# Attention probabilities transposed on TensorE: eight 128x128 transposes per unit, or sixteen in two row halves of the array

## The reference, cut to what matters

```python
scores = jnp.einsum('bhqd,bhkd->bhqk', q, k)
attn = jax.nn.softmax(scores / math.sqrt(DK), axis=-1)
out = jnp.einsum('bhqk,bhkd->bhqd', attn, v)
...
return out @ wo + bo
```

## Time and profile before

| | |
|---|---|
| time, median of 3 runs | 607.12 us (605.61 to 608.26) |
| the profiled execution | 603.87 us |
| its span, first to last instruction | 602.1 us |
| PE busy, PEld busy | 555.6 us (92%), 509.2 us (85%) |
| DVE, ACT, POOL busy | 459.0 us (76%), 302.1 us (50%), 335.5 us (56%) |
| mean granted clock of TensorE | 0.990 |

### The profile page before, as it was taken

How to read it: one execution, slowest core, us unless ns; L and a number is a source line. 1 busy time by engine, 2 the same in 40 slices (tenths; PEclk the granted TensorE clock), 3 DMA queues, 4 the chain that set the end, 5 groups by cost and what they waited for, 6 DMA issues and landing times.

```text
span 602.1 us, 22151 instructions
## 1 busy us (share of the span) xinstructions
PE 555.6 (92%) x9632; PEld 509.2 (85%) x9632; DVE 459.0 (76%) x902; ACT 302.1 (50%) x647; POOL 335.5 (56%) x665
## 2 busy tenths in 40 slices
PE   6699999999998999999999988899999989999984
PEld 6588798989897988988989878789898979898874
DVE  4977877777777767677767798888888878888862
ACT  6365666575866666557565742242322424222252
POOL 1613535354436353648457496877676555465635
PEclk9979999999999999999999998999999999999999
DMA  8900000000111100000000000000000000000000
GB/s 244 282 2 3 3 2 2 2 4 2 37 37 37 38 4 2 3 2 3 2 3 3 2 3 1 1 3 2 7 7 7 7 10 7 7 7 7 5 12 14
DMA packets 10975, 12.44 MB, mean 21 GB/s; under 512 B 1024, under 2 KB 8704, under 8 KB 10880
## 3 DMA queue, kind: packets, MB, share of 16 engines
q1 hardware_dynamic: 10880, 11.04, 6.2%
HBM read 9.99 MB, written 1.05 MB: 18 GB/s over the span
## 4 chain that ended last, share of the span: by engine, by line
PE 60%; DVE 19%; ACT 8%; POOL 8%; issue 4%; DMA 1%; SPq 0%; POOLq 0%; ACTq 0%; DVEq 0%
PE ps_p L366 10%; PE ps_p L481 10%; PE ps_p L367 8%; PE ps_p L368 8%; PE ps_s L395 5%; PE ps_o L410 5%; PE ps_p L455 3%; ACT probs L574 3%; DVE top L698 3%; DVE probs L721 3%; PE ps_p L503 2%; ACT vv L549 2%; DVE rope_b L655 2%; ACT headsT L568 2%; PE ps_s L388 2%
## 5 line engine op out<-in xcount | busy, mean ns | idle before, releaser
L568 ACT ACTIVATE headsT<-ps_o 128x512 f32<-128x512 f32 x96 | 52.2, 596 | 206.9 <-PE ps_o L410 206.9
L481 PE MATMUL ps_p<-wo,headsT 128*128 128x128 f32 x768 | 94.1, 276 | 2.3 <-ACT headsT L568 1.3
L481 PEld LDWEIGHTS ps_p<-wo,headsT 128*128 128x128 f32 x768 | 89.7, 192 | 3.6 <-DVE rope_a L655 1.5
L709 DVE TENSOR_REDUCE total<-probs 128x16 f32<-128x1024 f32 x48 | 58.4, 1216 | 36.2 <-ACT probs L574 36.2
L698 DVE TENSOR_REDUCE top<-ps_s 128x8 f32<-128x512 f32 x96 | 61.7, 685 | 26.3 <-PE ps_s L395 26.1
L847 POOL TENSOR_TENSOR small<-mv,epsilon 128x1 f32<-128x1 f32 x48 | 17.9, 374 | 113.0 <-DVE mv L691 111.8
L721 DVE TENSOR_TENSOR probs<-probs,rinv 128x512 f32<-128x512 f32 x96 | 68.2, 713 | 0.0
L574 ACT ACTIVATE probs<-probs 128x512 f32<-128x512 f32 x96 | 61.2, 638 | 12.7 <-DVE probs L702 12.7
L366 PE MATMUL ps_p<-xT_hi,wq_hi 128*128 128x256 f32 x192 | 59.5, 310 | 5.9 <-DVE xT_lo L642 3.3
L455 PE MATMUL ps_p<-eye,probs 128*128 128x128 f32 x384 | 53.9, 275 | 9.7 <-ACT vv L549 2.9
L549 ACT ACTIVATE vv<-ps_p 128x512 f32<-128x512 f32 x96 | 57.5, 599 | 9.3 <-PE ps_p L450 9.1
(11 more groups left out here) (144 smaller groups left out, 1480.3 us busy)
## 6 DMA issues: line engine op xcount, KB each, us to landing
out<-y_out SPq DMA_DIRECT2D x16, 64.0 KB, 1.5
X<-in_x SPq DMA_DIRECT2D x1, 768.0 KB, 8.0
across<-in_across SPq DMA_DIRECT2D x1, 704.0 KB, 10.4
wq_raw<-in_L_xattn_sa_wq SPq DMA_DIRECT2D x2, 256.0 KB, 3.1
wk_raw<-in_L_xattn_sa_wk SPq DMA_DIRECT2D x1, 512.0 KB, 5.1
wv_raw<-in_L_xattn_sa_wv SPq DMA_DIRECT2D x1, 512.0 KB, 7.7
wo<-in_L_xattn_sa_wo SPq DMA_DIRECT2D x1, 512.0 KB, 8.8
wo<-in_L_xattn_ca_wo SPq DMA_DIRECT2D x1, 512.0 KB, 10.1
```

The lines of the kernel that those rows point to most:

```text
L481: last = mm(bank[:, 0:E], headsT[:, p, :, :].rearrange("r b q -> r (b q)"), wo[:, layer % 2, p, :], start=(p == 0), stop=(p == PAIRS - 1))
L568: nc.scalar.activation(headsT[:, :, b, :], ps_o[b][:, :].rearrange("r (p q) -> r p q", q=S), ACT.Copy)\
```

## The change

The ring's wait is moved into a helper, and the two fills P0 and P1 are written by one loop. Instead of 8 transposes of 128 rows, each into one bank for a pair of heads, it issues 16 of 64 rows: batch 0 (rows 0 to 63) goes into one bank, batch 1 (rows 64 to 127) into the next, alternating. A bank then holds one batch of all eight pairs, where it held both batches of four pairs. Both banks must be free before the first transpose. The wait for the second half of the heads stands before the ninth, and both `filled` increments come with the last two. `weight_values` reads `probsT` at the new places; ScalarE's copies are the same.

```diff
-                            q = 128 * (p % HALF) + 64 * b
                             last = mm(ps_o[b][64 * c:64 * c + 64, 64 * p:64 * p + 64],
-                                      vv[of, w % 2, c, p, :], probsT[of, p // HALF, q:q + 64],
+                                      vv[of, w % 2, c, p, :], probsT[of, b, 64 * p:64 * p + 64],
                                       start=True, stop=True, skip_group_check=True)
...
+            def turn_probabilities(u, at):
+
+                banks = [ring(u, at + b) for b in range(2)]
+                for p in range(PAIRS):
+                    if p % HALF == 0:
+                        pe.wait_ge(normed, NORMED.at(u - 1, p // HALF))
+                    for b in range(2):
+                        of = slice(64 * b, 64 * b + 64)
+                        last = nc.tensor.transpose(banks[b][:, 64 * p:64 * p + 64],
+                                                   probs[of, (u - 1) % 2, 2 * p:2 * p + 2, :].rearrange("q h k -> q (h k)"),
+                                                   eye[of, of])
+                        if p == PAIRS - 1:
+                            last.then_inc(filled, 1)
...
-                elif name == "P":
-                    pe.wait_ge(normed, NORMED.at(u - 1, j))
-                    for pp in range(HALF):
-                        at_head = 2 * (HALF * j + pp)
-                        last = nc.tensor.transpose(bank[:, 128 * pp:128 * pp + 128],
-                                                   probs[:, (u - 1) % 2, at_head:at_head + 2, :].rearrange("q h k -> q (h k)"),
-                                                   eye[:, :])
...
-                    fill(u, at, name, j)
+                    if (name, j) == ("P", 0):
+                        turn_probabilities(u, at)
+                    elif name != "P":
+                        fill(u, at, name, j)
```

More of the change, by code:

```diff
@@ L408, in weight_values, with ring @@
                             of = slice(64 * g, 64 * g + 64)
-                            q = 128 * (p % HALF) + 64 * b
                             last = mm(ps_o[b][64 * c:64 * c + 64, 64 * p:64 * p + 64],
-                                      vv[of, w % 2, c, p, :], probsT[of, p // HALF, q:q + 64],
+                                      vv[of, w % 2, c, p, :], probsT[of, b, 64 * p:64 * p + 64],
                                       start=True, stop=True, skip_group_check=True)
                 last.then_inc(weighted, 1)
-            def fill(u, at, name, j):
+            def ring(u, at):
                 n = FILL.before(u) + at
-                bank = ps_p[n % BANKS]
                 if n >= BANKS:
@@ L424, in fill @@
                         pe.wait_ge(dve_emptied, EMPTY_D.at(was_u, was_name, was_j))
+                return ps_p[n % BANKS]
+            def turn_probabilities(u, at):
[10 more added lines that the diff above has]
+                            last.then_inc(filled, 1)
+            def fill(u, at, name, j):
+                bank = ring(u, at)
                 if name == "T":
```

## The result

The changed kernel takes 609.82 us (median of 20 runs) against 606.02 us for the kernel before (20 runs beside it): ratio 1.0059, 95% interval 1.0044 to 1.0074, 3.6 us slower. A ratio here is taken over all executions and lies nearer that of their averages than that of their medians, which are 3.8 us apart; one execution of e2, of 1042 us, is in none. The time lies in the range of the prediction, but the change cost four times the 0.9 us of the forecast.

The account below looks back on a forecast made before the run. Odd steps were taken as bound by the loop through the value product, ScalarE, V1's bank and K1, transposes beside it with 0.29 us to spare. Step effects summed to +0.9 us: 607.12 to 608.0 us, own range 606 to 610, wider 604.5 to 617.

Parts of the forecast that it names:

- Odd steps, "effect 0": Eleven odd steps without another stall: phase 0.12 us shorter, but the wait for ScalarE's copy of V1 grows as much; effect 0.
- pairs: Two half-height transposes, one per row half of the array, run beside each other and cost 58 ns together.
- entering: Change from the full array to the split shape ahead of the transposes: 0.09 us, hidden where a wait stands there.
- leaving: Change from the split shape back to the full array behind the transposes: 0.20 us.
- Even steps with one T: Twelve even steps (2 to 12, 34 to 44): phase ends 0.24 us later, within the 0.29 us to spare; effect 0.
- Steps 46 to 48: Last steps, without projections: two of them save 0.12 us each, -0.2 us together.
- Steps 18 to 28: Six even steps with two inputs in T: 0.22 us more behind the release, 0.10 us to spare; 6 x 0.12 = 0.7 us.
- Case D: Forecast's case with dearer changes of array shape, 0.40 us and more: even steps lose tenths each, +3 to +5 us; chance 0.05.
- Steps 14 and 30: Second half waits 1.1 us and more, nothing waits behind it: 2 x 0.22 = 0.4 us longer.
- step 32: Among fourteen steps with long waits behind the transposes: effect 0.
- The sum: All step effects together: +0.9 us, from 607.12 to 608.0 us.
- rival A: Phase doesn't get shorter because weight loads hold the pace, 0.87 to 0.93 us: +9.3 us, 616.4 us; chance 0.22.

Follow-up runs that it names:

- e2: Kernel before with the half-height transposes in odd steps only, full ones in even steps: 604.75 us, ratio to before 0.9969.
- e5: Kernel before with each transpose issued twice in eleven quiet odd steps (7 to 13, 17, 19, 37 to 45): 606.35 us, one execution, only its trace read.
- e9: Kernel before with half of the transposes left out in the eleven quiet odd steps: 607.00 us, one execution, only its trace read.
- e1: Full transposes of before, but both banks waited for ahead of the first and both fills reported behind the last: 609.28 us, ratio to before 1.0041.
- e3: Kernel before with the half-height transposes in even steps only: 610.09 us, ratio to before 1.0060.
- e4: Changed kernel with extra matmuls that nobody reads in idle stretches of steps 14 (7), 30 (13) and 32 (8): 2.1 us under the changed kernel.
- e7: Changed kernel with all sixteen transposes taken from batch 0, one row half of the array: 620.28 us, one execution, time not compared.
- e11: Changed kernel with the wait for the second bank moved behind the first transpose of batch 0: ratio to before 1.0023.
- e10: Kernel before, full transposes everywhere, with extra matmuls that nobody reads in steps 3, 5, 14, 15, 16, 30, 31 and 32: ratio to before 0.9905.

## Why the prediction was nearly right, and where it was not

*Odd steps, "effect 0":* right, for the reason given. The wait for V1's copy ends last whatever the transposes take, within 0.29 us (e5, e9). That the phase itself is 0.12 us shorter there can't be read, since V0's copy holds K0 at 4.51 us. The terms of the sum came out well: pairs at 62 ns for 58, entering 0.10 us for 0.09, leaving about 0.20 for 0.20.

*Even steps with one T, 0:* nearly; 0.09 us each. In step 42 Q0's second matmul comes 0.37 us later instead of 0.24, which uses up the 0.29 us and 0.08 more.

*Steps 46 to 48, -0.2 us:* they gave nothing but the missing pause of step 46.

*Steps 18 to 28, "6 x 0.12 = 0.7 us":* 2.1 us. The step that failed is the start: I let the phase begin 0.11 us behind VectorE's end, as the fifth transpose does in before, but the first transpose behind V begins 0.26 us behind it, in the full shape too (e1). That is 0.15 us of each step. The phase itself came out as forecast, 0.65 us from its first transpose to Q0 where I had 0.66, but the half that it replaces had taken less than my 0.44: to Q0's second matmul it is 0.28 us more than before where I had 0.22. With 0.09 us to spare, that makes the 0.35. The entry does hide in the wait, as I had it. Case D of the rivals gives a time near the measured one by changes of shape of 0.40 us and more; they cost about 0.30, so its number is no merit of its mechanism.

*Steps 14 and 30, "2 x 0.22 us":* 2.0 and 1.9 us in the profile, and step 32 as much, where I had 0. Where the clock stays up they lose 0.43 us (step 14 of e3) and 0.28 (both in e4), near the forecast; the rest is the clock, which the prediction left out of the sum without a reason. Behind a fall matmuls run 0.21 us apart instead of 0.12 for a while. The granted clock had shown a fall in step 31 of before, behind an idle stretch of 1.97 us, and I had not asked what longer stretches would do. The falls are not the change's alone, though: step 30 falls in four of five kernels whose even steps are those of before, and step 14 in two of five with the early wait and nothing to fill it (changed and e7; not e1, e3, e11). The Trainium skill (TensorE: Matmul & The Clock Gate, section Why this matters for your kernels) warns of idle gaps between bursts of matmuls; the traces agree in that most falls stand behind such gaps and none was left where all eight were filled, but the same gap had a fall in one trace and none in another.

*The sum:* +0.9 us forecast, +3.6 us measured over twenty runs. By the traces the slower even steps, less what the feed-forward steps absorb, are some 2.3 us, steps 14 and 30 without the clock 0.7, and the pauses that moved give back 1.8; that leaves some 2.4 us for the clock, an estimate. The executions bear out its direction: the mean granted clock is 0.980 in twenty of the changed kernel and 0.986 in 64 of before, and at equal clock the changed kernel is only 0.7 to 0.9 us slower on average (608.2 against 607.4 us at 0.983 and 0.984, 609.9 against 609.1 at 0.979 to 0.981). That goes with the clock and is no experiment on it. e4, with matmuls in three of the steps, is 2.1 us under the changed kernel.

*Luck:* the time stands inside my range of 606 to 610 in part because the start of the sum, the median of three executions, was 1.1 us above that of twenty. The wider range up to 617 came from rival A, which e7 refutes.

## What to carry to other kernels

Look behind the work that is made shorter for the wait that ends last; if it is one that the work does not feed, shortening the work only lengthens the wait, and any wait moved forward to allow it is a loss. A wait moved ahead of work that used to fill it has more than one price: the delay, a later start behind the wait (0.23 us instead of 0.08 here), and what a longer idle stretch can do to TensorE's clock. Matmuls that nobody reads, in eight idle stretches, were worth more than the edit (e10 is 0.95% under before, part of it from pauses that moved). One profile is not enough to lay a clock fall at a change's door: look whether kernels that leave the step alone have it too. And before an experiment's number is put down to the new part, look for the same number in the experiment that leaves that part out: e1 had the 0.23 us all along.

## What the runs showed of the hardware that was not expected

- A row-split fp32 transpose of 64 rows by 128 columns takes 62 ns in one half of the array (e7), and the two halves, writing different banks as they do here, overlap: a pair takes 62 ns too.
- The first transpose's load behind a wait for VectorE starts 0.23 us behind the release, in the full-array shape (e1) as in the half-height one (changed kernel), against 0.08 us when four transposes have gone ahead (before) and 0.12 us when one has (e11).
- Entering the half-height shape costs 0.10 us where no wait stands ahead of it (step 19) and nothing visible behind one; leaving it costs about 0.20 us.
- The granted clock fell to half mostly behind idle stretches of 1.6 to 3.3 us, in some traces and not in others, in the same step behind the same stretch (2.12 us in step 16: not in before, but in e9). In step 23 of e2 it fell behind none over 1.3 us.
- Pauses of 0.4 to 1.5 us in TensorE's stream that belong to no wait; one stands at the same matmul in four kernels with the same number of records ahead of it.
